# First normalisation on ScalarE in the preparation, its parts inside the build, two turning loads ahead of the last store, weight factors inside the SAGE layers

## What is computed

```python
edge_index = stack([src, dst])
h = maximum(layernorm(x), 0.0)
x = x + sage(h)      # two convolutions: relu(conv1(h)), then conv2
h = maximum(layernorm(x), 0.0)
x = x + gcn(h)       # sums weighted by edge_weight, then a bias
h = maximum(layernorm(x), 0.0)
x = x + inter(h)     # messages with edge features, a three-layer MLP, two norms
h = maximum(layernorm(x), 0.0)
x = x + maxk(h)      # largest 32 of 256 features kept, then a mean

def sage_conv(h):    # W_l, b_l, W_r: weights of 256 x 256
    agg = segment_sum(h[src], dst) / maximum(deg, 1)[:, None]
    return agg @ W_l + b_l + h @ W_r
```

## Time and profile before

| | |
|---|---|
| median of 3 runs | 1837.4 us (1836.95 to 1838.09) |
| the profiled execution | 1835.88 us, span 1834.0 us |
| TensorE busy | 1628.2 us, 89% |
| VectorE busy | 1101.0 us, 60% |
| ScalarE busy | 669.6 us, 37% |
| GpSimd busy | 353.9 us, 19% |
| DMA, mean rate | 134 GB/s |

### The profile page before, as it was taken

The page is one execution under the profiler, slowest core; times in us unless marked ns, Lnnn a source line. Parts: engine busy times, 40 slices in busy tenths (PEclk is TensorE's granted clock), DMA queues, the critical chain, the costliest instruction groups (busy, mean ns, idle before and its releaser), DMA issues.

```text
span 1834.0 us, 43434 instructions
## 1 busy us (share of the span) xinstructions
PE 1628.2 (89%) x10959; PEld 1205.1 (66%) x10960; DVE 1101.0 (60%) x3560; ACT 669.6 (37%) x1742; POOL 353.9 (19%) x923
## 2 busy tenths in 40 slices
PE   2888888888871999998998899999989999986996
PEld 1334444343330877777887788888878888864885
DVE  5899999999996122122333666666644777775111
ACT  0777887787762111111111122222213444441000
POOL 0555555555543000000000000000001211110000
PEclk7899999999995999999999899999989999997998
DMA  1566566566564655652335356656532222221444
GB/s 42 147 158 167 130 166 159 130 171 154 130 178 117 178 162 165 175 179 90 125 125 172 105 158 173 172 154 189 149 92 90 75 74 74 74 73 36 144 152 151
DMA packets 353541, 245.56 MB, mean 134 GB/s; under 512 B 195242, under 2 KB 337382, under 8 KB 353510
## 3 DMA queue, kind: packets, MB, share of 16 engines
q1 hardware_dynamic: 353510, 245.19, 46.6%
HBM read 138.17 MB, written 99.31 MB: 129 GB/s over the span
## 4 chain that ended last, share of the span: by engine, by line
issue 62%; PE 16%; DVE 9%; POOL 4%; DVEq 4%; POOLq 3%; DMA 1%; SPq 0%; ACT 0%; ACTq 0%
PE ps L1307 8%; PE ps L1380 8%; DVE e_buf L914 2%; POOL work L616 2%; POOLq L582 2%; DVE e_buf L917 2%; DVE e_buf L915 2%; POOL e_buf L585 1%; DVEq L914 1%; DVEq L917 1%; DMA wgt_blocks<-arena 1%; DVEq L928 0%; DVE work L1050 0%; POOL w_col L581 0%; DVE arena L1061 0%
## 5 line engine op out<-in xcount | busy, mean ns | idle before, releaser
L1380 PE MATMUL ps<-arena 128*128 128x256 f16 (+1 forms) x5000 | 604.0, 274 | 53.5 <-POOL arena L606 43.5
L1380 PEld LDWEIGHTS ps<-arena 128*128 128x128 f16 x5000 | 488.1, 98 | 149.8 <-issue 81.5
L1307 PE MATMUL ps<-e_buf 128*128 128x400 bf16 (+1 forms) x2476 | 429.6, 310 | 66.4 <-DVE e_buf L917 27.7
L1307 PEld LDWEIGHTS ps<-e_buf 128*128 128x128 bf16 x2476 | 201.8, 98 | 294.4 <-DVE e_buf L917 95.1
L1374 PE MATMUL ps<-arena 128*128 128x256 f32 x1250 | 281.1, 382 | 0.0
L1374 PEld LDWEIGHTS ps<-arena 128*128 128x128 f32 x1250 | 238.0, 192 | 31.3
L616 POOL TENSOR_TENSOR work<-work 128x256 f32<-128x256 f32 x75 | 54.9, 731 | 1014.0 <-ACT work L775 1014.0
L917 DVE TENSOR_SCALAR e_buf<-iota,off_g,front 128x400 bf16<-128x400 f16 (+1 forms) x619 | 230.9, 373 | 0.0
L915 DVE TENSOR_SCALAR e_buf<-iota,front 128x128 bf16<-128x128 f16 x619 | 210.5, 340 | 0.0
L914 DVE TENSOR_SCALAR e_buf<-iota,front 128x128 bf16<-128x128 f16 x619 | 162.1, 262 | 36.5 <-PE ps L1307 27.3
L589 POOL TENSOR_SCALAR e_buf<-e_buf,w_col 128x128 bf16<-128x128 bf16 x200 | 94.8, 474 | 133.6 <-DVE e_buf L914 133.5
(11 more groups left out here) (195 smaller groups left out, 1711.3 us busy)
## 6 DMA issues: line engine op xcount, KB each, us to landing
arena<-turned_blocks SPq DMA_DIRECT2D x75, 800.0 KB, 4.3
wgt_blocks<-arena SPq DMA_DIRECT2D x25, 1600.0 KB, 10.2
arena<-wgt_blocks SPq DMA_DIRECT2D x25, 1600.0 KB, 8.3
cnt_blocks<-work SPq DMA_DIRECT2D x25, 800.0 KB, 5.5
turned_blocks<-arena SPq DMA_DIRECT2D x25, 800.0 KB, 3.5
e_raw<-edge_features_padded SPq DMA_DIRECT2D x25, 576.0 KB, 7.9
edge_features_padded<-in_edge_attr SPq DMA_DIRECT2D x24, 512.0 KB, 9.8
out<-arena SPq DMA_DIRECT2D x24, 128.0 KB
```

The source lines that it names most:

```text
L1307: return pe.matmul(bank[:, 0:wide], sets_of(par, u, part), q_of(par, u), start=start, stop=True, skip_group_check=True)
L1380: m = pe.matmul(agg[par][:, 0:wide], BLK16[par][:, b * P:(b + 1) * P], ZH[zin(i)][:, b * ZW + part * D:b * ZW + part * D + wide], start=(b ...
```

## The change

- **Where X lies.** The scratch of the preparation moves from the start of `arena` to the region `o_z1`, so X can be loaded right behind the edge lists. POOL sets X's padding at once, and SP issues the loads of X ahead of the early weights.
- **The statistics and the normalised rows on ScalarE.** While VectorE runs its preparation chain, ScalarE makes the row sums (25 activations with an accumulated output), the negative means, the sums of squared deviations (25 more) and the roots. When the chain is over, VectorE takes the reciprocals, GpSimd makes a factor and a shift for each row (two operations on 128x25), and ScalarE writes 25 tiles of R_ in one pass: Relu(X * factor + shift). Only after that does ScalarE begin its part of the build.
- **The two parts inside the build.** In each of the 25 chunks ScalarE makes one tile's first part (after set 3) and GpSimd one tile's second part (after set 6).
- **SP.** The first two turning loads move ahead of the last `store` with its `pad_edges`; they wait for the stores of counts so far.
- **SAGE factors.** `largest` and the bias step stay at the end of the build; `across` and `powers` move into round 1 of SAGE1 on VectorE, TensorE's steps into rounds 0 and 1. VectorE no longer waits there for the stores of weights; ScalarE does, in round 1.
- **Factors of the later layers.** `largest` of both matrices goes ahead of SAGE2's first block on VectorE, `across` (now one for both) behind it, and `powers` ahead of SAGE2's last block.

The diff, cut to its core:

```diff
-        rows = region(0, 3 * EB * P).rearrange("p (a c e) -> p a c e", a=3, c=EB)
+        rows = region(o_z1, PREP).rearrange("p (a c e) -> p a c e", a=3, c=EB)
...
SP:
+            sp.wait_ge(s_xpad, 1)
+            for j, at in enumerate(range(0, NT, SB)):
+                n = min(SB, NT - 1 - at)
+                sp.dma_start(X[:, at:at + n, :], x[at * P:(at + n) * P, :].rearrange("(n p) d -> p n d", p=P)
+                             ).then_inc(s_x[j], 16)
...
             with sp.Fori(0, NPAIR) as j:
                 for c in range(2):
                     store(j * 2 + c, c)
+            def load_turned(n, par):
+                sp.dma_start_transpose(BLK16[par].rearrange("p (b d) -> p b d", d=P),
+                                       cnt_dram[bass.ds(n * P, P), :]).then_inc(s_blk[par], 16)
+            sp.wait_ge(s_prep, PREP_STEPS)
+            for b in range(2):
+                sp.wait_ge(s_store_c[b], 16 * NPAIR)
+                load_turned(b, b)
             store(NT - 1, 0)
...
                 if i == 0:
-                    load(0, 0, 0, 0)
-                    load(1, 1, 0, 1)
                     with sp.Fori(1, NT // 2) as j:
                         keep(j * 2 - 2, j - 1, 0)
                         load(j * 2, j * 2, j, 0)
...
POOL:
+            pool.wait_ge(s_rs, 1)
+            chain(pool.tensor_scalar(h_all, rs_all, H_SCALE, None, ALU.mult))
+            pool.tensor_tensor(shift_all, nmean_all, h_all, ALU.mult).then_inc(s_rs, 1)
...
                 for i in range(PER):
                     weigh_pair(c, i, packed[i])
+                    if i == 6:
+                        second(c)
...
ACT:
+            for j in range(NT // SB):
+                act.wait_ge(s_x[j], 16 * (1 + (j == NT // SB - 1)))
+                for n in range(j * SB, (j + 1) * SB):
+                    m = act.activation(R_[:, n, :], X[:, n, :], ACT.Copy, accum_out=row_sum[:, n:n + 1])
+            m.then_inc(s_mean, 1)
+            act.wait_ge(s_mean, 1)
+            act.activation(nmean_all, row_sum, ACT.Copy, scale=-1.0 / D).then_inc(s_mean, 1)
+            act.wait_ge(s_mean, 2)
+            for n in range(NT):
+                m = act.activation(R_[:, n, :], X[:, n, :], ACT.Square, bias=nmean_all[:, n:n + 1],
+                                   accum_out=sq_all[:, n:n + 1])
+            m.then_inc(s_var, 1)
+            act.wait_ge(s_var, 1)
+            act.activation(sd_all, sq_all, ACT.Sqrt, bias=eps_outer, scale=1.0 / D).then_inc(s_std, 1)
+            act.wait_ge(s_rs, 2)
+            for n in range(NT):
+                act.activation(R_[:, n, :], X[:, n, :], ACT.Relu, bias=shift_all[:, n:n + 1],
+                               scale=h_all[:, n:n + 1]).then_inc(s_zD, 1)
             act.wait_ge(s_prep, PREP_STEPS)
             start_walk(act, mybir.EngineType.Activation)
             chunk(0, 0, 0)
...
DVE, end of the preparation:
+            dve.wait_ge(s_std, 1)
+            dve.reciprocal(rs_all, sd_all).then_inc(s_rs, 1)
...
DVE, behind the build:
-            across(0, 2, 1)
...
-            for j in range(NT // SB):
-                dve.wait_ge(s_x[j], 16 * (1 + (j == NT // SB - 1)))
-                for n in range(j * SB, (j + 1) * SB):
-                    dve.bn_stats(bn_all[:, n, :], X[:, n, :])
...
+            dve.wait_ge(s_z2, NT)
             for par in range(2):
-                for s in (s_store_c, s_store_w):
-                    dve.wait_ge(s[par], 16 * ((NT + 1 - par) // 2))
+                dve.wait_ge(s_store_c[par], 16 * ((NT + 1 - par) // 2))
...
             def sage1(n, g, par, half, at0, at1, at2):
+                if isinstance(n, int) and n == 1:
+                    conv_scales()
...
+            largest(1, 4, wk(late["W_maxk"], 2 * D)[:, :, 0:D])
             largest(2, 4, wk(late["W_msg"], D))
...
+            row_phase(PH_SAGE2, pre_sage2, post_sage2, early=late_largest, late_step=late_powers)
...
PE:
-            spread_largest(8, 0, (4, 5))
...
-            row_layer(1, wk(late["W_gcn"], D), 19, 23)
-            spread_largest(SCALE_CONV + 4, 1, (4,))
-            spread_largest(SCALE_CONV + 14, 2, (4,))
+            row_layer(1, wk(late["W_gcn"], D), 19, 23, early=late_largest, late_step=late_spread)
```

More of the change, by code:

```diff
@@ L649, in weigh_pair, with first_part @@
                     act.reg_add(k_reg, k_reg, 1)
+            def first_part(n):
+                wait(act, s_zD, n + 1 + CR)
+                act.activation(span(ZH[0], n * ZW, D), node(R_, n), ACT.Copy).then_inc(s_z0, 1)
             def chunk(c, half, par):
@@ L986, in row_phase @@
                 pre(0, g0, g0 % 2)
+                if early:
+                    early()
                 def body(n, g, h, par):
+                    if late_step and isinstance(n, int) and n == NT - 1:
+                        late_step()
                     if beside:
@@ L992, in body @@
                     post(n - 1, g - 1, 1 - par)
-                tiles(dve, phase, body, first=1, peel=1 if beside else 0)
+                tiles(dve, phase, body, first=1, peel=1 if beside or late_step else 0)
                 post(NT - 1, g0 + NT - 1, (g0 + NT - 1) % 2)
@@ L1425, in body @@
                     aggregate(i, n, q, h, par, c1, NT)
-                tiles(pe, i, body, first=1)
+                tiles(pe, i, body, first=1, peel=1 if late_step else 0)
                 g = g0 + NT - 1
```

149 lines of the change are left out of this document (69 added, 80 removed).

## The result

| | kernel before | changed kernel |
|---|---|---|
| median of four runs | 1837.74 us | 1807.47 us (1806.83 to 1807.95) |
| ratio, 95% interval | | 0.9835 (0.9818 to 0.9852) |
| profiled execution, its span | 1835.9, 1834.0 us | 1807.95, 1806.2 us |
| ScalarE's first weighting to the last store's issue | 49.73 to 542.68: 493.0 us | 59.88 to 558.65: 498.8 us |
| SAGE1: first product; `rdeg_conv`, the VectorE step behind it | 591.01, 838.17 | 558.68, 820.46 |

The forecast was 1808.0, in a range of 1795 to 1822.

A forecast was written before the change was run, and what follows sets the result against it. TensorE (busy 89%) was taken as the bound, its main idle stretch between build and SAGE1. 1835.9 + 11.0 + 4.5 - 36.8 + 0.8 - 9.1 = 1806.3 us, forecast 1808 us as median, range 1795 to 1822.

The forecast's parts named there:

- Part 1: Ahead of the build: ScalarE's Relu pass and table load start the build 11.0 us later, ends 6.5 and 13.
- Part 2: Inside the build: GpSimd's 25 subtractions slow VectorE, a cost of 4.5 us, ends 0 and 17.
- rival 2: In the build, GpSimd blocks VectorE for each whole subtraction: 17 us instead of 4.5, 1820.5 us; chance 12%.
- Part 3: Gap behind the build: 38.6 us gained despite a 10.2 us stand before block 2, 1.8 back for clock, net 36.8.
- Rival 1: Behind the build: no stand before block 2, gain 48.8 us instead of 36.8, 1796 us; chance 14%.
- Part 4: Later layers' factors: 0.8 us cost inside SAGE2, 9.1 us gain ahead of GCN, ends 7.8 and 10.
- the allowance of 1.5 us for the median: In the sum: the median of the runs lies 1.5 us above the profiled execution, so 1806.3 becomes 1808 us.
- Rivals 3 and 4: Build loses a set per chunk, 62 us, 1865 us, 5%; early turning loads delay the last store, 1815 us, 12%.

The follow-up runs named there:

- best_gap: `best` with GpSimd's whole subtraction moved up two instructions within the seventh pair, where GpSimd idles: 1791.7 us, ratio 0.9745 to the kernel before.
- the halves: GpSimd's subtraction of each chunk cut into two of 128 columns: 1807.3 us in the changed kernel, 1791.1 us in `best`.
- factors_only: The kernel before with only the weight-factor steps moved into the SAGE layers: 1832.8 us, ratio 0.9966 to the kernel before.
- late_apart: The changed kernel with SyncE's eleven late weight loads issued one at a time behind later turning loads of SAGE1: 1805.5 us, ratio 0.9831 to the kernel before.
- late_and_waits: `late_apart` with SyncE's waits for the last weight block's store and padded edge features also moved behind SAGE1's turning loads: 1802.4 us, ratio 0.9803 to the kernel before.
- best: The changed kernel with the edits of `relu_in_build` and `late_and_waits` together: 1790.5 us, ratio 0.9746 to the kernel before.
- dve_shift: The changed kernel with 32 useless semaphore increments added to VectorE's program behind the build: 1807.4 us, ratio 0.9832 to the kernel before.
- relu_in_build: The changed kernel with ScalarE's 25 Relu activations moved from ahead of the build into it, one per chunk: 1796.1 us, ratio 0.9778 to the kernel before.

## Why the prediction was right, point by point

**Part 1 (11.0 forecast, 10.15 measured).** The step held: 0.49 us a tile, 12.39 for the pass. The load of ScalarE's table registers cost nothing behind the pass (the first weighting starts 0.50 us after the last tile did, no more than from tile to tile), which are the 0.9 us too many. The sums ended at 36.2, inside the range given.

**Part 2 (4.5 forecast, 5.8 measured, 7.3 against the same kernel without it).** That VectorE pays, and is the pace, was right. The size was too small, and how the loss comes about was read wrongly: I had made it a share of GpSimd's time (0.2 from rows 7, 0.37 from rows 5, and 0.26 taken), and it isn't one. These are a subtraction of the changed kernel, and one of `best_gap`:

```profile
554.17 0.75 DVE L942 TENSOR_SCALAR e_buf<-iota,off_g,front 128x200 bf16<-128x200 f16 x1
554.18 0.67 POOL L591 TENSOR_TENSOR arena<-arena  x1
...
554.84 0.24 DVE L939 TENSOR_SCALAR e_buf<-iota,front 128x128 bf16<-128x128 f16 x1
```

```profile
540.68 0.72 DVE L949 TENSOR_SCALAR e_buf<-iota,front 128x128 bf16<-128x128 f16 x1
540.69 0.66 POOL L600 TENSOR_TENSOR arena<-arena  x1
```

The usual 0.32 and 0.30 us have become 0.75 and 0.72. In all 25 chunks of the changed kernel a VectorE operation starts within 0.011 us of the subtraction and ends 0.05 to 0.07 us after it, whether its usual length is 0.24 or 0.32 us; the next one has its usual length again. So a subtraction of 0.65 us costs VectorE 0.36 to 0.47 us (0.43 in the median), what is left of it beyond the one operation's own length. Times 25 that is 10.7 us, of which the build loses 7.3. It also says why the halves brought nothing: each of the 50 holds one operation too, for 0.14 to 0.23 us, 9.3 us in sum. Rows 7 show the same, L915 ending 0.06 us after L590: what rival 2 called "slowed by half, not stopped" was an operation held to GpSimd's end. Its mechanism is nearer to the rows than a share is; its price is not. By the rule of the Trainium skill, page "SBUF — State Buffer", section "Who interferes with whom", that I weighed in Part 2 the build would have lost 16.3 us; the trace agrees that the operation isn't done before GpSimd's, but VectorE lost 0.43 us and not 0.65 each time. One caution: the builds without the subtractions took 491.5, 493.0 and 495.4 us (the last in `factors_only`, with nothing changed in it), those with them 497.7 to 500.0, so what the build as a whole pays is known to about 2 us.

**Part 3 (38.6 and 1.8 back forecast, 38.5 and 1.9 measured).** Behind the build's end nearly everything came within 0.4 us on the forecast's scale (the positions less the 15.97 by which the last store was later): block 1 ended at 557.1 for 557.5, and block 2 started at 567.9 for 567.7. Only the store of turned block 0 was issued 1.1 us late (556.9 for 555.8), and it made that up by moving faster than worked out (5.5 us to the turning load for 6.5). (The 1.8 was itself a slip: 9.62 less 7.9 is 1.7.) But the step that named the cause was half right. I had the late weights alone hold the store of turned block 0; `late_apart` and `late_and_waits` show SyncE's wait for the last weight block behind them, and a store that moves slowly behind that. Rival 1 ("no stand") would not have come by taking the queue away, and I had not seen it. The margin of the last store was 2 us, as said, and it was not late.

**What was not in the forecast** is VectorE's wait for its program, 2.2 to 2.4 us of TensorE. It has no step in the sum. The range covered it, by luck as far as this wait goes.

**Part 4 (0.8 and 9.1 forecast, 0.9 and 9.7 measured).** Right; `factors_only` repeats 0.8 and 8.6 in the kernel before. That chain hid completely.

**The sum.** At `rdeg_conv` I had forecast 21.3 us less and it was 17.7, 3.6 short: 1.3 from the build and 2.4 from VectorE's program, 0.2 from part 3, less the 0.9 that part 1 gave back; 0.6 stay open. Part 4 gave 0.6 back and about 1.2 more came behind it, mostly between GCN's start and MAXK (MAXK's first product 1679.23 and 1651.68, 27.55 less, where GCN's first edge product had 26.6); I did not look for its cause. So the profiled execution ran at 1807.95 for 1806.3, and the median is 0.5 us off by luck: the allowance of 1.5 us for the median wasn't needed and covered what had been missed. Rivals 3 and 4 are out: the build grew by 0.23 us a chunk, not 2.5, and the early loads cost the last store nothing.

**A better kernel.** `best` at 1790.5 us is 17 us below the changed kernel. Not tried is `best` with the subtractions behind the build; with the turning loads free there, I can't tell from these runs whether the 7 us of the build or the 15 us in the open weigh more. Nor did any run change VectorE's program in `best`, where its wait still costs TensorE 2.1 us.

## What to carry to other kernels

Work taken off an open stretch should go into the engine with room inside the long loop, not into a pass ahead of it: the same 25 activations cost 11 us there and nothing here. Before a move is priced, look at what else holds the same point: the stand before block 2 had two holds in a row and a slow store behind them, each visible only when the one ahead was gone, and the same stand made a subtraction in the open cheaper than one hidden in the build. And a wait in the profile names who came last, not who sets the pace: 11.7 us of waits for GpSimd went away without moving the end. What did set it showed in the operations of two kernels laid side by side.

## What the runs showed of the hardware

- **A VectorE operation that starts with a GpSimd subtraction of 128x256 f32 (0.65 us) ends just behind it**, 0.05 to 0.07 us after, 25 times of 25, instead of after its own 0.24 to 0.32 us; the rows stand under part 2.
- **An activation with an accumulated output** is followed by an instruction of its own, which overlaps the next: 128x256 copies start 0.40 us apart instead of 0.31.

```profile
13.71 0.40 ACT L678 ACTIVATE arena<-arena 128x256 f32<-128x256 f32 x1
14.02 0.19 ACT L678 ACTIVATION_READ_ACCUMULATOR arena<-arena 128x1 f32 x1
14.11 0.40 ACT L678 ACTIVATE arena<-arena 128x256 f32<-128x256 f32 x1
```

- **An engine's program comes by DMA**, and VectorE can stand for it behind a wait: 2.8 us where the queues are quiet, 7 us where they move 366 GB/s. That it is the program is inferred, from the one packet of the queue "instruction" ahead of it and from `dve_shift`, where 32 added instructions moved the place by two blocks.
- **A stand of 2 us can be followed by the lower clock as well.** In `relu_in_build`, behind the 2.1 us stand for VectorE's program, the granted clock was 0.60 from 588.5 to 592.5 us, where eight products took 3.19 us instead of 1.90; in `late_apart` the same eight took 3.27 us behind it. In the changed kernel and in `late_and_waits` the same stand had no such tail. These are the busy times and clocks of two stretches (columns as in rows 1):

```profile
585.00:588.50 3.50, 1.39 (x12) 1.24 (x13) 2.19 (x7) 0.60 (x1) 0.00 (x0) 0.97 1.17 281
588.50:592.50 4.00, 4.00 (x16) 3.12 (x15) 0.00 (x0) 0.00 (x0) 0.00 (x0) 0.60 0.39 157
```
